# Down products one block behind the up products in a mixture-of-experts loop, and one residual loaded early

## The reference

```python
x = x + gnn(layernorm(x))          # segment_sum over edges, relu(h @ W1 + b1) @ W2 + b2
xt = layernorm(x)                  # T = 2500 rows, D = 512
gate = softmax(xt @ Wg)            # E = 8 experts
topv, topi = top_k(gate, 2)
topv = topv / (sum(topv) + 1e-6)
scores = zeros((T, E)).at[arange(T)[:, None], topi].set(topv)
out = zeros_like(xt)
for e in range(E):
    h = gelu(xt @ W1[e] + b1[e])   # hidden size 256
    ye = h @ W2[e] + b2[e]
    out = out + ye * scores[:, e:e + 1]
x = x + out
```

## Time and profile before

| | us |
|---|---|
| median of 3 runs | 651.04 (650.71 to 652.23) |
| the profiled execution | 650.67 |
| its span in the trace | 648.7 |
| TensorE busy | 563.2 (87% of the span) |
| VectorE busy | 465.6 (72%) |
| ScalarE busy | 281.5 (43%) |
| GpSimd busy | 285.9 (44%) |

### The profile page before, as it was taken

One profiled execution on the slowest core, in us unless ns is written; L12 is line 12 of the kernel. 1 busy time (PEld: TensorE's weight loads), 2 busy tenths in 40 slices (PEclk: granted clock), 3 DMA queues, 4 the chain that ended last, 5 costly groups with the idle time before them and its releaser, 6 DMA issues.

```text
span 648.7 us, 13456 instructions
## 1 busy us (share of the span) xinstructions
PE 563.2 (87%) x4500; PEld 417.3 (64%) x4501; DVE 465.6 (72%) x979; ACT 281.5 (43%) x539; POOL 285.9 (44%) x237
## 2 busy tenths in 40 slices
PE   5788989999899999999999999704899999999970
PEld 3688979666566766766766665704676776766650
DVE  4788788883699999898996422777975555555562
ACT  3464767332442362335232302531565555555552
POOL 4362322130083463446423524235466666666643
PEclk9899899998999999999999999955999999999995
DMA  8253300300123333423232134945977777777755
GB/s 251 86 142 115 81 1 1 76 1 1 46 86 104 98 105 114 120 86 103 81 96 81 49 96 84 398 132 157 283 132 131 137 133 134 130 133 130 133 84 74
DMA packets 39572, 71.71 MB, mean 111 GB/s; under 512 B 12193, under 2 KB 16433, under 8 KB 38850
## 3 DMA queue, kind: packets, MB, share of 16 engines
q0 software_dynamic: 11328, 25.55, 21.9%
q1 hardware_dynamic: 21351, 31.08, 15.2%
q10 hardware_dynamic: 6834, 14.34, 6.9%
HBM read 43.46 MB, written 29.06 MB: 112 GB/s over the span
## 4 chain that ended last, share of the span: by engine, by line
PE 57%; DVE 23%; ACT 7%; issue 7%; DMA 3%; DVEq 1%; SPq 1%; POOL 1%; ACTq 1%; POOLq 0%; PEldq 0%
PE psum L1533 22%; PE psum L1517 8%; PE psum L1687 7%; PE psum L1447 6%; PE psum L1572 6%; PE psum L1677 5%; ACT he L893 3%; DVE he_lo L1370 3%; DVE hot_lo L1123 2%; DVE hot_key L1123 2%; DVE he_hi L1369 2%; DMA src_i<-in_src 2%; PE psum L1425 1%; DVE stat L936 1%; DVE y L1381 1%
## 5 line engine op out<-in xcount | busy, mean ns | idle before, releaser
L1123 DVE TENSOR_TENSOR hot_key<-iota_key,key_w 128x1200 f16<-128x1200 f16 x125 | 106.4, 851 | 28.0 <-PE psum L1517 27.0
L714 ACT ACTIVATE counts<-psum 128x400 bf16<-128x400 f32 x125 | 62.1, 507 | 139.3 <-PE psum L1517 137.9
L1533 PE MATMUL psum<-counts,z_hi 125*128 125x500 bf16 x400 | 102.2, 376 | 2.4 <-ACT h L741 1.7
L653 POOL DMA_INDIRECT out_x<-y,target_i x47 | 76.9, 1636 | 62.1 <-ACT y L884 41.4
L1533 PE MATMUL psum<-counts,z_lo 125*128 125x500 bf16 x400 | 101.4, 376 | 0.0
L1517 PE MATMUL psum<-hot_key,hot_lo 128*128 128x200 f16 x750 | 82.5, 249 | 4.0 <-DVE hot_lo L1123 2.2
L1123 DVE TENSOR_TENSOR hot_lo<-iota_lo,lo_w 128x768 f16<-128x768 f16 x125 | 85.1, 681 | 0.0
L1517 PEld LDWEIGHTS psum<-hot_key,hot_lo 128*128 128x128 f16 x750 | 66.1, 98 | 24.5 <-issue 3.7
L893 ACT ACTIVATE he<-psum,eb_col,up_undo 128x128 f32<-128x128 f32 x94 | 42.7, 457 | 87.3 <-PE psum L1677 42.9
L619 POOL TENSOR_TENSOR xt<-xt_whole,xt 125x512 f16<-125x512 f32 x20 | 50.7, 2537 | 47.3 <-DVE xt L1163 39.0
L623 POOL TENSOR_TENSOR x_res<-x_res,b_row 125x512 f32<-125x512 f32 x20 | 31.4, 1579 | 88.8 <-DMA x_res<-in_x 88.8
(11 more groups left out here) (272 smaller groups left out, 1132.1 us busy)
## 6 DMA issues: line engine op xcount, KB each, us to landing
x_res<-in_x SPq DMA_DIRECT2D x20, 224.0 KB
out_x<-x SPq DMA_DIRECT2D x20, 224.0 KB
xt_d<-xt SPq DMA_DIRECT2D x20, 224.0 KB
up_raw<-in_L_ffn_W ACTq DMA_DIRECT2D x8, 512.0 KB, 4.1
up_d<-up_split ACTq DMA_DIRECT2D x8, 512.0 KB
w_both<-up_d SPq DMA_DIRECT2D x8, 512.0 KB, 8.1
w_raw<-in_L_ffn_W SPq DMA_DIRECT2D x8, 512.0 KB, 9.3
W_raw<-in_L_gnn_W ACTq DMA_DIRECT2D x2, 1024.0 KB, 5.7
```

The source lines that it names most:

```text
L653: pool.indirect_dma_start(out=out[:, :], in_=y[:, k % YB], in_offset=None, out_offset=bass.IndirectOffsetOnAxis(ap=target_i[:, k:k + 1], a ...
L714: act.activation(counts[:, it % 2, :, place:place + W], psum[:, WIN + w % 2, 0:MW].rearrange("p (w h) -> p h w", w=W), ACT.Copy).then_inc( ...
L1123: ins = dve.tensor_tensor(hot[:, w % RING].rearrange("p s (n two) -> p s n two", two=2), iota[:].rearrange("p (o n two) -> p o n two", o=1 ...
L1533: ins = mm(psum[:, AGG + c, 0:GN], half[:, t, c * 128:(c + 1) * 128], counts[0:P, g % 2, t], start=(t == 0 and n == 0), stop=(t == T - 1 a ...
```

## The change

Part 1. TensorE's round k is now up(k), transposes of block k+1, down(k-1). Round 0 multiplies down a block of zeros (`he_hi` and `he_lo` are set to zero by VectorE ahead of the loop, and counts of `he_ready`, `gelu_ready`, `y_taken` and `down_done` start one block higher), and behind the loop stands one more down for the last block in use. The last block of an expert is multiplied down in the first round of the next, so w2_hi, w2_lo and w2_raw become one tensor each for all experts, and TensorE computes the place in them from its loop's register. `up` gets a wait for `gelu_ready`, as banks 2 and 3 are written a round ahead. VectorE's round is: expert's number, `turned_low(k+1)`, split of he(k), landings or `split_low`, sum of block k-1. ScalarE scales block k-2.

Part 2. The residual of the last tile has a tensor of its own, `x_last`, loaded on SyncE's queue behind the loop over groups, ahead of `up_undo`; it counts on `eb_in`, for which GpSimd's `rest_of_sum` of tile 19 and VectorE wait at 48. `load_residual(G - 1, 3)` between the stores goes.

```diff
@@ SyncE
+            sp.dma_start(x_last[:], x[(T - 1) * P:T * P, :]).then_inc(S["eb_in"], 16)
             sp.wait_ge(S["up_out"], 32 * NE)
...
             store(G - 2, 3)
-            load_residual(G - 1, 3)
             store(G - 1, 0)
@@ GpSimd
             def rest_of_sum(g, q):
-                pool.wait_ge(res_in[q], 32 * (g + 1))
-                pool.tensor_tensor(x_res[:, q], x_res[:, q], b2_row[:], ALU.add).then_inc(S["res_sum"], 1)
+                if 4 * g + q < T - 1:
+                    pool.wait_ge(res_in[q], 32 * (g + 1))
+                else:
+                    pool.wait_ge(S["eb_in"], 48)
+                rows = x_res[:, q] if 4 * g + q < T - 1 else x_last[:]
+                pool.tensor_tensor(rows, rows, b2_row[:], ALU.add).then_inc(S["res_sum"], 1)
@@ ScalarE
-                act.wait_ge(S["y_taken"], k + 2)
+                act.wait_ge(S["y_taken"], k + 3)
...
+            act.sem_inc(S["gelu_ready"], HC)
...
-                        act.wait_ge(S["he_ready"], HC * (k - 1) + m + 1)
+                        act.wait_ge(S["he_ready"], HC * k + m + 1)
...
-                if k >= 1:
-                    scale_rows(k - 1)
+                if k >= 2:
+                    scale_rows(k - 2)
...
-            scale_rows(NB - 1)
+            for k in (NB - 2, NB - 1):
+                scale_rows(k)
@@ VectorE
+            step(dve.memset(he_hi[:].bitcast(F32), 0.0))
+            dve.memset(he_lo[:].bitcast(F32), 0.0).then_inc(S["he_ready"], HC)
...
+            def sum_rows(k, of):
+                if k >= YB:
+                    dve.wait_ge(y_out[k % YB], 16 * (k // YB + 1))
+                if k == 0:
+                    dve.wait_ge(S["b2_in"], 16)
+                dve.wait_ge(S["down_done"], k + 2)
+                dve.tensor_tensor(y[:, k % YB], psum[:, 4], b2_all[:, bass.ds(of, 1)].rearrange("p o d -> p (o d)"), ALU.add).then_inc(S["y_taken"], 1)
+
+            dve.sem_inc(S["y_taken"], 2)
             dve.wait_ge(S["slots_known"], BLOCKS)
             for k in range(NB):
                 expert = dve.value_load(expert_i[0:1, k:k + 1], min_val=0, max_val=NE - 1)
+                turned_low(k + 1)
                 for m in range(HC):
-                    dve.wait_ge(S["gelu_ready"], HC * k + m + 1)
-                    if k >= 1:
-                        dve.wait_ge(S["down_done"], k)
+                    dve.wait_ge(S["gelu_ready"], HC * (k + 1) + m + 1)
+                    dve.wait_ge(S["down_done"], k + 1)
                     step(dve.tensor_copy(he_hi[:, m], he[:, m]))
                     dve.tensor_tensor(he_lo[:, m], he[:, m], he_hi[:, m].bitcast(F32), ALU.subtract).then_inc(S["he_ready"], 1)
-                turned_low(k + 1)
                 if k == 0:
                     landings()
                 if 1 <= k < NE - 1:
                     split_low(k + 1)
...
+                if k >= 1:
+                    sum_rows(k - 1, summed)
+                summed = expert
+            sum_rows(NB - 1, summed)
@@ TensorE
+            def up(k, e):
+                pe.wait_ge(S["xT_ready"], k * 2 + 2)
+                pe.wait_ge(S["gelu_ready"], k * 2 + HC)
...
+            def down(ready, taken, of):
+                trio = [(he_hi, w2_hi), (he_hi, w2_lo), (he_lo, w2_hi)]
+                for m in range(HC):
+                    pe.wait_ge(S["he_ready"], ready + m)
+                    if m == 0:
+                        pe.wait_ge(S["y_taken"], taken)
+                    for n, (h_, w_) in enumerate(trio):
+                        ins = mm(psum[:, 4], h_[:, m], w_[:].rearrange("p e m n -> p (e m n)")[:, bass.ds(of + m * D, D)], start=(m == 0 and n == 0), stop=(m == HC - 1 and n == 2))
+                ins.then_inc(S["down_done"], 1)
...
                 with pe.Fori(start, end) as k:
...
+                    up(k, e)
                     turn(k + 2, bass.ds((k + 1) & (XB - 1), 1))
...
+                    down(k * 2 + 1, k + 1, (e - 1) * HC * D + ((k - start + 63) & 64) * (HC * D // 64) if e else 0)
                 start = end
+            down(start * 2 + 1, start + 1, (NE - 1) * HC * D)
```

More of the change, by code:

```diff
@@ L217, in gnn_moe @@
         h1_lo = sb("h1_lo", [128, KC, GN], F32R)
-        sb("apart_too", [128, 784], F32)
+        sb("apart_too", [128, 272], F32)
+        x_last = sb("x_last", [P, D], F32)
         x_res = sb("x_res", [P, 4, D], F32)
@@ L236, in gnn_moe @@
         sb = allocator(ffn)
[L237 to L244, removed]
+        w1_both = [sb(f"w1_both_{e}", [128, 2, KC, H], F16) for e in range(NE)]
+        w2_hi = sb("w2_hi", [128, NE, HC, D], F32R)
+        in_place = ExitStack()
+        w2_raw = allocator(in_place)("w2_raw", [128, NE, HC, D], F32)
+        in_place.close()
+        w2_lo = sb("w2_lo", [128, NE, HC, D], F32R)
         sb("apart_four", [128, 40], F32)
@@ L1146, in residual @@
                 step(dve.tensor_tensor(x2[:, q].rearrange("p (b n) -> p b n", b=2), psum[0:P, bank:bank + 2, 0:DH],
-                                       x_res[:, q].rearrange("p (b n) -> p b n", b=2), ALU.add))
+                                       (x_res[:, q] if n < T - 1 else x_last[:]).rearrange("p (b n) -> p b n", b=2), ALU.add))
                 step(dve.bn_stats(ln2[:, q % 2, 0:6], x2[:, q]))
@@ L1333, in _ @@
             turned_low(0)
-            dve.wait_ge(S["eb_in"], 32)
+            dve.wait_ge(S["eb_in"], 48)
             dve.tensor_scalar(up_undo[:].bitcast(I32), up_undo[:].bitcast(I32), -1, (254 - UP) << 23, ALU.mult, ALU.add).then_inc(S["undo_ready"], 1)
@@ L1653, in turn @@
                         rows = xg[:, place, h, c * 128:(c + 1) * 128]
-                        ins = mm(psum[:, h, c * 128:(c + 1) * 128], rows if place == 0 else rows.rearrange("p o d -> p (o d)"), ident16[:], start=True, stop=True)
+                        ins = mm(psum[:, h, c * 128:(c + 1) * 128], rows if isinstance(place, int) else rows.rearrange("p o d -> p (o d)"), ident16[:], start=True, stop=True)
                     ins.then_inc(S["turned"], 1)
@@ L1665, in _ @@
             pe.wait_ge(S["slots_known"], BLOCKS)
+            def up(k, e):
+                pe.wait_ge(S["xT_ready"], k * 2 + 2)
+                pe.wait_ge(S["gelu_ready"], k * 2 + HC)
+                trio = [(0, xT_hi), (1, xT_hi), (0, xT_lo)]
+                for m in range(HC):
+                    cols = slice(m * 128, (m + 1) * 128)
+                    for c in range(KC):
+                        for i, (half, x_) in enumerate(trio):
+                            ins = mm(psum[:, 2 + m, 0:B], w1_both[e][:, half, c, cols], x_[:, c], start=(c == 0 and i == 0),
+                                     stop=(c == KC - 1 and i == 2))
+                    ins.then_inc(S["up_done"], 1)
+            def down(ready, taken, of):
+                trio = [(he_hi, w2_hi), (he_hi, w2_lo), (he_lo, w2_hi)]
+                for m in range(HC):
+                    pe.wait_ge(S["he_ready"], ready + m)
[4 more added lines that the diff above has]
+                ins.then_inc(S["down_done"], 1)
             start = 0
@@ L1670, in _ @@
                 with pe.Fori(start, end) as k:
-                    pe.wait_ge(S["xT_ready"], k * 2 + 2)
-                    trio = [(0, xT_hi), (1, xT_hi), (0, xT_lo)]
-                    for m in range(HC):
-                        cols = slice(m * 128, (m + 1) * 128)
-                        for c in range(KC):
-                            for i, (half, x_) in enumerate(trio):
-                                ins = mm(psum[:, 2 + m, 0:B], w1_both[e][:, half, c, cols], x_[:, c], start=(c == 0 and i == 0),
-                                         stop=(c == KC - 1 and i == 2))
-                        ins.then_inc(S["up_done"], 1)
-                    turn(k + 2, bass.ds((k + 1) & (XB - 1), 1))
-                    trio = [(he_hi, w2_hi), (he_hi, w2_lo), (he_lo, w2_hi)]
-                    for m in range(HC):
-                        pe.wait_ge(S["he_ready"], k * 2 + (m + 1))
-                        if m == 0:
-                            pe.wait_ge(S["y_taken"], k + 1)
-                        for n, (h_, w_) in enumerate(trio):
-                            ins = mm(psum[:, 4], h_[:, m], w_[e][:, m], start=(m == 0 and n == 0), stop=(m == HC - 1 and n == 2))
-                    ins.then_inc(S["down_done"], 1)
+                    up(k, e)
+                    turn(k + 2, bass.ds((k + 1) & (XB - 1), 1))
+                    down(k * 2 + 1, k + 1, (e - 1) * HC * D + ((k - start + 63) & 64) * (HC * D // 64) if e else 0)
                 start = end
+            down(start * 2 + 1, start + 1, (NE - 1) * HC * D)
             with pe.If(start < NB):
```

17 lines of the change are left out of this document (5 added, 12 removed).

## The result

The changed kernel is slower, by 1.9%: 663.84 us median of 4 runs (658.38 to 666.15) against 650.88 (649.44 to 652.23, 4 runs), ratio 1.0193, 95% interval 1.0148 to 1.0237, which holds 1.02 too. Forecast were 642.8, within 637.5 to 651.5: wrong in sign, and the time lies outside the range. The profiled execution took 666.15, the longest of the four, with a span of 664.1; its parts add up to 15.4 more than in the span of before, 2.3 of which the median doesn't have.

The account below looks back on a forecast made before the run. TensorE's 3.32 us of work plus 0.66 waiting for he's split set each 3.98 us round, to become 3.60. Loop -13.3, start +4.1, end +3.3 and +0.6, early load -2.9 make -8.2: 642.8 us, range 637.5 to 651.5.

Parts of the forecast that it names:

- the register that addresses W2: Loop, TensorE ahead of down: address computed behind the wait for y, put at 0.02 us a round, at most 0.1.
- rival C: Loop: TensorE's register work ahead of down exposed by 0.18 more, round 3.78, +7.6, 650.4 us; chance 0.12.
- 0.39: Loop: time from the end of down(k-1) to VectorE's first instruction, 0.39 us a round.
- the split: Loop: VectorE's he_hi, he_lo, he_hi, he_lo up to the instruction behind, 0.94 us a round.
- y to TensorE: Loop: from the end of the sum y to TensorE's down, 0.05 us a round.
- The start: Loop's first rounds: split_low on the path, five rounds of 4.74 us, up(8) later by 4.1 us.
- The end: Behind up(43): two downs 3.60 apart, 3.3 us more; the last add 0.6 us later.
- Part 2: Ahead of the token list: early load of the last residual saves 2.9 us, between 1.4 and 4.2.
- A: Loop: he_hi runs into GpSimd's add, 0.30 more a round, +12.6, 655.4 us; chance 0.09.
- B: Loop: round stays at 3.98 for another limit, landings of adds, +16.0, 658.8 us; chance 0.04.
- D: Loop: VectorE's path shorter than summed, TensorE bounds the round at 3.32, -11.8, 631.0 us; chance 0.05.
- E: Loop: an add holds VectorE's port for all its time, round 4.95, +56.7, 699.5 us; chance 0.02.

Follow-up runs that it names:

- e1: The changed kernel again, unaltered, on a second chip: 662.30 us, ratio 1.0335 to the kernel before.
- e8: The changed kernel with W2's place kept in a register of its own, one register instruction behind the wait in place of three: 650.48 us, ratio 0.9986.
- e2: The changed kernel with a constant address of W2, so seven blocks are multiplied with another expert's W2: 642.39 us, ratio 1.0036.
- e7: The changed kernel with each expert's first block written out ahead of its loop, so W2's address is constant: 645.96 us, ratio 0.9954.
- e5: The kernel before, unaltered, profiled on another chip: 649.99 us.
- e4: The changed kernel without the early load of the last residual: 664.12 us, ratio 1.0346.
- e9: e7's kernel with the sum y ahead of split_low and the leave for up(0) given ahead of ScalarE's waits for the scores: 640.18 us, ratio 0.9850.
- e3: The kernel before with only the early load of the last residual: 638.19 us, ratio 0.9974.
- e6: The kernel before, old order and no early load, with down's W2 addressed by a register expression as in the changed kernel: 652.59 us, ratio 1.0033.
- e11: The kernel before with the early load of the last residual and the eight experts' ends loaded ahead of the loops: 649.54 us, ratio 0.9989.
- e12: e3's kernel (the kernel before with only the early load) run again on the chip of another group: 647.82 us, ratio 0.9969.
- e10: e9's kernel with TensorE loading the eight experts' ends into registers ahead of the loops: 642.98 us, ratio 0.9882.

## Why the prediction was wrong

**The step that failed** is the register that addresses W2. It was put at 0.02, with 0.1 as its upper bound, and rival C gave it 0.20 in all; it measures 0.33 (after, e1), 0.25 - 0.15 = 0.10 with one instruction (e8), and is gone without (e2, e7). Over the 35 rounds that is 11.6 of the 12.7 us by which the loop fell short; e1 against e2 puts it at 19.9 us for the whole kernel, with what follows from it. The reasoning was from the transposes, whose eight register addresses cost nothing. But their registers are computed while matmuls queued ahead are still running: a row of the profile of before, which the prediction didn't read (the transposes' instructions in the round of the earlier trace rows), has them from 542.0 on, while the first transpose starts at 542.54:

```profile
L1654 PEldq FUSED_REGOPS  x7: 46/46/46, 542.0 to 542.7; - x7
```

Behind a wait nothing is queued, and each instruction is seen in full. The prediction counted one register for what were three instructions, and took the nearest row by kind and not by place.

**The round otherwise** came out as summed. Without the register it is 3.62 (e7) and 3.53 (e2) where 3.60 was foreseen: 0.39 was 0.27, the split, y and down were right within 0.02, and y to TensorE is 0.15 where 0.05 was taken from he_lo's end to down.

**The gain to be had** was read from one chip. 0.38 a round nearly holds where the second Gelu is late (e5 to e7: 0.33), but a part of it was that lateness, which the sum took for the chain itself; the profile of before had it to see, in six of the 35 rounds that take 3.61. On the chip of e1 to e4 the old rounds took 3.72 on average, the new ones without the register 3.53, and with the costs of start and end e2 only ends even with before (1.0036).

**The start** cost 8.3, not 4.1. The rounds with split_low were right: 4.72 to 4.85 in e7, against 4.74; with the register they took 5.08 to 5.35. Missed were 1.5 on the way to up(0), whose leave (gelu_ready) stood behind ScalarE's waits for the scores (a semaphore instruction that the prediction didn't place in its queue; e9 takes it out and gains 1.5), and 0.7 up to up(1), which is gone in e9 too.

**The end**: 3.6 for the two downs, 3.3 foreseen. The last add comes 1.7 later, not 0.6. y of block 46 starts 8.45 behind the last down, near the foreseen 8.2, but three adds then stand one behind the other, 1.86 apart, in GpSimd's timeline of after:

```profile
650.51 1.55 POOL L656 DMA_INDIRECT out_x<-y,target_i  x1 [1.60 <-ACT y L887]
652.37 1.55 POOL L656 DMA_INDIRECT out_x<-y,target_i  x1 [0.30 <-ACT y L887]
654.23 1.55 POOL L656 DMA_INDIRECT out_x<-y,target_i  x1 [0.30 <-issue]
```

**Part 2** gave 2.0 to 2.2 of the 2.9 foreseen, inside its range, in each pair of profiles. The stall in front of the last residual (3.56 in the earlier trace rows) is 1.44 in e3, and its releaser in the timeline of e3 is a DMA of the stores, as foreseen for what is late next:

```profile
426.51 0.69 DVE L1151 TENSOR_TENSOR x<-psum,x_last 125x512 f32<-125x512 f32 x1 [1.44 <-DMA xt_d<-xt]
```

Its landing was put 2.2 earlier than the old start; it came 1.2 earlier (19.62 behind the first of the last_lo and not 20.83). In after the residual has no idle time in front: from 413 on TensorE, which had stood still for 0.68 us ahead of 412.48, ran for some 3 us at the lower of its two clocks (0.50 is 1.2 GHz; stage, columns as above), and VectorE's work in front came 1.56 later than in before. Still the residual starts at 19.59, the same place, so that the landing may bound it there too; no run takes the two apart.

```profile
413.82:415.82 2.00, 2.00 (x11) 2.00 (x10) 0.80 (x2) 0.30 (x1) 0.00 (x0) 0.50 1.04 398
```

**The sum** of what was missed, in the profiled execution: 12.7 in the loop, 4.2 at the start, 0.3 and 1.1 at the end, 0.8 in part 2, 0.5 behind the last add, and 4.0 ahead of all that, where nothing was changed: 23.6, from -8.2 to +15.4.

**The rivals.** C was right in place and wrong in size: 0.33 for the register where it had 0.20. A is real on one chip (e1, 4.6 us) and rare on the first; in e7 17 of 70 he_hi are stretched, by 2.9 us in all, 16 of them beside a gather. B, D and E didn't come. E held VectorE's work to the end of the add; in the round of after shown above he_lo starts at 540.82 and y behind it at 541.03, within an add from 540.15 to 541.79, and they take their 0.29 and 0.68. The prediction also gave the rule of the Trainium skill (SBUF — State Buffer, "SBUF: two separate sides") too widely: there an operation with two SBUF inputs is held up only by a GpSimd operation that reads SBUF; whether the add counts as one no run shows, so that he_lo need not speak against the rule. What does is he_hi, which is held to 1.11 behind the add's start and not to its end, 1.59 behind (below).

## What to carry to other kernels

Register work behind a wait is on the path in full, some 0.11 us for each sequencer instruction; count the instructions that the address expression becomes, not the registers, and compute them ahead of the wait or unroll to constants. When an order is turned, list each instruction of each queue that moves onto the new path: a leave given behind a foreign wait and a long instruction ahead of the sum cost as much here as the loop had to give. And see on more than one chip that the idle time you mean to remove is what you take it for: a stall that lies beside another (e6, e11) makes single edits read as worth nothing.

## What the runs showed of the hardware that was not expected

- 0.10 to 0.11 us for each register instruction of TensorE's sequencer behind a wait, of which 32 to 64 ns show in its row.
- A load of a register from memory on TensorE's sequencer: 0.30 in its row, 0.64 from one to the next (e10).
- In the profiles of before, e5 and e12 TensorE's signal behind the second half of up comes late beside GpSimd's add, by 0.35 to 0.39 in the median of 28 or 29 rounds of 35, and ScalarE's second Gelu with it; in e3, on another chip, in none (0.014). It makes 7.6 us of 638 to 648. The cause is open: the first Gelu starts within the same add undisturbed (544.23 in one from 543.68).
- he_hi takes 0.54 when it starts 0.58 behind the start of an add and 0.38 at 0.73 behind (e1), 0.43 at 0.61 behind that of a gather (e7), in place of 0.23; right behind it he_lo and y take what they always do. Whenever it starts, a stretched he_hi ends at one place: 1.11 to 1.13 behind the start of the add in all 24 of e1, 1.03 to 1.04 behind that of the gather in all 16 of e7. One that starts 0.5 or 1.04 behind the add's start takes its 0.23.
